# The score mask moves from TensorE to ScalarE, and the weighing of the values to another place in TensorE's order

## The reference

```python
def attn_layer(x, Wqkv, qs, ksc, Wo):        # 16 heads of 64
    q, k, v = split(shift_tokens(x) @ Wqkv)
    q, k = l2norm(q) * qs, l2norm(k) * ksc    # then rotary embedding of both
    # windows of 32 queries against 64 keys (the window before and their own)
    sim = where(mask, -max, (q @ k.T) * 8.0)
    return softmax(sim) @ v @ Wo
def ffn_layer(x, ...):                       # 128 -> 2 x 341 -> 128
    return (a * gelu(gate)) @ W2 + b2        # of the layer norm of shift_tokens(x)
x = attn_layer(x) + x;  x = ffn_layer(x) + x
```

## Time and profile before

| | |
|---|---|
| median of 3 runs | 3490.75 us |
| the profiled execution | 3489.94 us |
| its span | 3488.1 us |
| mean granted TensorE clock | 0.983 |
| PE busy | 3326.3 us (95%) |
| PEld busy | 2681.4 us (77%) |
| DVE busy | 2632.2 us (75%) |
| POOL busy | 2606.3 us (75%) |
| ACT busy | 2200.0 us (63%) |
| mask matmul L903 | 384 of 379 ns |
| split of a weight block on POOL L398 | 72 of 1292 ns |
| gate's table load L639 | 48 of 1283 ns |

### The profile page before, as it was taken

How to read it: one execution, slowest core, us unless ns; L and a number is a source line. 1 busy time by engine, 2 the same in 40 slices (tenths; PEclk the granted TensorE clock), 3 DMA queues, 4 the chain that set the end, 5 groups by cost and what they waited for, 6 DMA issues and landing times.

```text
span 3488.1 us, 149929 instructions
## 1 busy us (share of the span) xinstructions
PE 3326.3 (95%) x63806; PEld 2681.4 (77%) x63806; DVE 2632.2 (75%) x4403; ACT 2200.0 (63%) x4154; POOL 2606.3 (75%) x2894
## 2 busy tenths in 40 slices
PE   6999999999999999999789999999999999999997
PEld 4777778777777777877667777777777778778875
DVE  3777777877787877777458787778787778777773
ACT  3666666666666666666436666666666666666664
POOL 5877787787787777787348778877877877777772
PEclk8999999999999999999879999999999999999998
DMA  2222221221221222221112222212212212221111
GB/s 81 70 55 52 64 56 52 64 61 48 63 62 49 61 62 53 62 63 45 30 26 72 55 54 65 57 51 63 61 47 64 62 51 66 55 56 47 52 46 35
DMA packets 117856, 195.41 MB, mean 56 GB/s; under 512 B 23756, under 2 KB 36552, under 8 KB 117192
## 3 DMA queue, kind: packets, MB, share of 16 engines
q1 hardware_dynamic: 117192, 185.82, 19.6%
HBM read 33.71 MB, written 1.05 MB: 10 GB/s over the span
## 4 chain that ended last, share of the span: by engine, by line
PE 72%; POOL 16%; ACT 6%; issue 3%; DVE 1%; POOLq 0%; DMA 0%; ACTq 0%; SPq 0%; DVEq 0%
PE o_ps L946 10%; PE tr L961 8%; PE s_ps L917 7%; PE tr L930 5%; PE qk_ps L857 5%; POOL rotated L419 5%; PE qk_ps L859 4%; POOL rotated L448 4%; PE qk_ps L858 4%; PE f_ps L1007 4%; PE tr L884 4%; PE tr L857 3%; PE tr L897 3%; POOL prob L425 3%; ACT sq L527 2%
## 5 line engine op out<-in xcount | busy, mean ns | idle before, releaser
L419 POOL TENSOR_TENSOR rotated<-rotated 128x1024 f32<-128x1024 f32 x384 | 917.7, 2390 | 23.7 <-DVE rotated L705 23.7
L448 POOL TENSOR_TENSOR rotated<-rotated,rn 128x1024 f32<-128x1024 f32 x384 | 731.0, 1904 | 30.1
L425 POOL TENSOR_TENSOR prob<-prob,rden 128x512 f32<-128x512 f32 x384 | 436.6, 1137 | 417.2 <-DVE rden L737 413.4
L699 DVE TENSOR_TENSOR rotated<-qk_ps,rot 128x1024 f32<-128x1024 f32 x384 | 469.8, 1223 | 368.0 <-ACT sq L527 362.8
L705 DVE TENSOR_TENSOR rotated<-qk_ps,rot 128x512 f32<-128x512 f32 x768 | 490.4, 679 | 0.0
L917 PEld LDWEIGHTS s_ps<-kt,qt 64*32 64x32 f32 x24576 | 359.5, 107 | 139.6 <-issue 139.6
L712 DVE TENSOR_REDUCE ss_floor<-sq 128x16 f32<-128x1024 f32 x384 | 463.9, 1208 | 0.0
L573 ACT ACTIVATE ot<-o_ps 128x512 f32<-128x512 f32 x384 | 230.6, 601 | 317.4 <-PE o_ps L946 317.4
L917 PE MATMUL s_ps<-kt,qt 64*32 64x64 f32 x24576 | 421.5, 218 | 0.0
L543 ACT ACTIVATE qt<-tr 128x512 f32<-128x512 f32 x384 | 230.1, 599 | 294.5 <-PE tr L884 291.5
L961 PE MATMUL tr<-ot,wo 128*128 128x128 f32 x3072 | 414.6, 278 | 0.0
(11 more groups left out here) (151 smaller groups left out, 6960.5 us busy)
## 6 DMA issues: line engine op xcount, KB each, us to landing
vs<-vn SPq DMA_DIRECT2D x384, 192.0 KB
vs<-vtail SPq DMA_DIRECT2D x384, 64.0 KB, 2.5
vtail<-vn SPq DMA_DIRECT2D x384, 64.0 KB, 2.2
staging<-layer_wqkv_dram SPq DMA_DIRECT2D x72, 256.0 KB, 3.7
wo<-layer_wo_dram SPq DMA_DIRECT2D x12, 512.0 KB, 4.6
xs<-xa SPq DMA_DIRECT2D x48, 128.0 KB, 2.3
fs<-xa SPq DMA_DIRECT2D x48, 128.0 KB, 2.6
xs<-xa SPq DMA_DIRECT2D x48, 127.8 KB, 3.2
```

The lines of the kernel that those rows point to most:

```text
L419: nc.gpsimd.tensor_tensor(rot_c[h], rot_c[h], rot_s[h], ALU.add).then_inc(rot_added, 1)
L425: nc.gpsimd.tensor_tensor(prob[h][:, :, :], prob[h][:, :, :], rden[h][:, :].unsqueeze(2).to_broadcast([P, 2 * PAIRS, KEYS]), ALU.mult).the ...
L448: nc.gpsimd.tensor_tensor(folded, folded, rn[:, :].unsqueeze(2).to_broadcast([P, 2 * UH, DH]), ALU.mult).then_inc(qkn_ready, 1)
L699: nc.vector.tensor_tensor(rot_c[h], src, part(0, 0, DH), ALU.mult)
```

## The change

The mask of all units but the first of each pass is written by ACT: a copy of the bf16 mask, broadcast over the four pairs, into the score bank, behind the exponential of the unit before. PE's `scores` waits for it and adds onto it. The first unit of a pass keeps the mask matmul. On PE the values of unit n-2 are weighed between the key transposes and the values' projection of slot n; before, those of n-1 were weighed at the end of the slot. On ACT the order of a slot becomes exponential, mask, first guess, squares, queries, keys, outputs, values, transposed probabilities. On DVE `add_output` moves behind `differences`.

```diff
         @block.scalar
+            def place_mask(U):
+                act.wait_ge(dif_ready, ONE + U)
+                nc.scalar.activation(s_ps[:, :].rearrange("p (a k) -> p a k", a=PAIRS),
+                                     mask[:, min(U // 2 % TPS, 1), :].unsqueeze(1).to_broadcast([P, PAIRS, 2 * KEYS]), ACT.Copy
+                                     ).then_inc(mask_ready, 1)
...
                     if live(p, n) and after_gated:
                         queries(n)
                         keys(n)
-                    if live(p, n - 2):
-                        outputs(n - 2)
                     if live(p, n - 1):
                         exps(n - 1)
+                    if live(p, n) and n > p * UPP:
+                        place_mask(n)
+                    if live(p, n + 1):
+                        first_guess(n + 1)
+                    if live(p, n + 2):
+                        squares(n + 2)
                     if live(p, n) and not after_gated:
                         queries(n)
                         keys(n)
-                    if live(p, n + 2):
-                        squares(n + 2)
-                    if live(p, n + 1):
-                        first_guess(n + 1)
+                    if live(p, n - 2):
+                        outputs(n - 2)
                     if live(p, n):
                         values(n)
...
         @block.vector
                     if live(p, n + 2):
                         rotate(n + 2)
-                    if live(p, n - 2):
-                        add_output(n - 2)
                     if live(p, n):
                         row_maxima(n)
                         differences(n)
+                    if live(p, n - 2):
+                        add_output(n - 2)
...
         @block.tensor
-            def mask_scores(U):
-                pe.wait_ge(dif_ready, ONE + U)
-                nc.tensor.matmul(s_ps[:, :], ident16[:, :],
-                                 mask[:, min(U // 2 % TPS, 1), :].unsqueeze(1).to_broadcast([P, PAIRS, 2 * KEYS]),
-                                 start=True, stop=False, skip_group_check=True)
-
             def scores(U):
                 h, t = U % 2, U // 2 % TPS
+                if U % UPP == 0:
+                    nc.tensor.matmul(s_ps[:, :], ident16[:, :], mask[:, 0, :].unsqueeze(1).to_broadcast([P, PAIRS, 2 * KEYS]),
+                                     start=True, stop=False, skip_group_check=True)
+                else:
+                    pe.wait_ge(mask_ready, ONE + U - U // UPP)
                 pe.wait_ge(kt_ready, ONE + U + 1)
...
                     if live(p, n):
                         query_heads(p, n)
                         key_heads(p, n)
-                        mask_scores(n)
+                    if live(p, n - 2):
+                        weigh_values(n - 2)
+                    if live(p, n):
                         project_v(n)
                         scores(n)
...
                     if live(p, n - 2):
                         project_out(p, n - 2)
-                    if live(p, n - 1):
-                        weigh_values(n - 1)
```

More of the change, by code:

```diff
@@ L199, in build @@
         s_ready = sem("s_ready")
+        mask_ready = sem("mask_ready")
         max_ready = sem("max_ready")
@@ L488, in _ @@
             for released in (sq_ready, qt_ready, kt_ready, prob_ready, pt_ready, vn_ready, ot_ready, fd_ready, fsq_ready,
-                             fn_hi_ready, gate_ready, guess_ready):
+                             fn_hi_ready, gate_ready, guess_ready, mask_ready):
                 act.sem_inc(released, ONE)
```

## The result

The changed kernel takes 3338.12 us (median of 4 runs, 3337.16 to 3340.91) against 3491.06 us for the kernel before in the same comparison: the ratio is 0.9567, 95% interval 0.955 to 0.9583, 153 us faster. The forecast was 3357 us. The profiled execution took 3337.87 us, its span is 3336.1 us, the mean granted clock 0.984.

What follows compares the result with a forecast made beforehand. It took a ring of waits among ACT, PE and DVE to bound the changed kernel: eight slots sum to 66.33 us against 69.11, 2.78 less, times 48 is 133 us, giving 3357 us; range 3285 to 3445.

Steps and rivals of the forecast that it cites:

- slots 0 and 1: Slots with the gated product and the down projection: forecast at 11.27 and 9.58 us from squares to squares.
- the variances and the spread: FFN work putting 0.92 us on PE in slots 4 and 6, forecast at 7.46 us each.
- the ring: Waits among ACT, PE and DVE, from squares through query copy, scores, maxima, square sums and guess to next squares: 7.15 us.
- the plain slot: One unit's slot without FFN work: forecast at 7.15 us from squares to squares, against 7.29 before.
- rival 1: PE's order alone counts, the guess isn't late: 64.2 us per iteration, 3256 us in all; chance 0.1.
- PE's own sum: PE's work in one slot after the change, if nothing else bound: 6.82 us, 0.47 less than 7.29.
- The centring: Slot 3: centring matmuls on PE take 1.12 us, their ACT copies start at 6.03; slot 8.42 us.
- Guess to squares: On ACT, from the first guess to the next squares: 0.41 us, two small instructions.
- The POOL wait: Probability transposes wait 68.7 us in 80 places for POOL's scaling, 1.43 us per iteration; should vanish.
- The mask's copy: ACT writing the mask into the score bank: taken as 0.60 us, 381 times; no cost in a plain slot.
- Rival 3: Slower: ACT's mask far dearer than a copy; 3668 us at 2.0 us, decides from 1.54 us; chance 0.1.
- Rival 2: The ring is 0.2 us a slot longer than summed, 77 us back: 3434 us; chance 0.15.

Runs made afterwards that it cites:

- e3: The changed kernel with DVE's output addition ahead of the row maxima again, nothing else: 3842.55 us, ratio 1.103 to the kernel before.
- e4: The changed kernel with ACT's first guess moved behind queries and keys, so the squares come ahead of it: 3297.52 us, ratio 0.945 to the kernel before.
- e5: The changed kernel with ACT copying the mask twice, the first time into a spare tile: 3390.53 us.
- e1: The changed kernel with the mask a matmul on PE again, all orders as changed: 3330.85 us, ratio 0.9544 to the kernel before.
- e2: The changed kernel with PE weighing the values of unit n-1 at the slot's end again: 3692.33 us, ratio 1.0583 to the kernel before.

## Why the prediction was right

The span of 8 units, squares to squares, in the changed kernel (squares start at 1099.09 in slot 0, then at 1112.84, 1120.04, 1127.28, 1135.58, 1142.93, 1150.31, 1157.67 and 1165.05):

| slots | forecast | measured |
|---|---|---|
| 0 and 1 (gated, down) | 20.85 | 20.95 |
| 2 | 7.28 | 7.24 |
| 3 (centring) | 8.42 | 8.30 |
| 4 | 7.46 | 7.35 |
| 5 | 7.43 | 7.38 |
| 6 | 7.46 | 7.36 |
| 7 | 7.43 | 7.38 |
| sum | 66.33 | 65.96 |

Against the kernel before the gain isn't spread evenly. There the same distances are, by their medians over the span, 22.16 us for slots 0 and 1, then 7.29, 8.26, 8.21, 7.29, 8.55 and 7.29 for slots 2 to 7. So slots 0 and 1 gain 1.2 us, slot 4 0.9 and slot 6 1.2; slots 2 and 3 stay within 0.05, and slots 5 and 7 are 0.09 us slower. In slots 4 and 6 the variances and the spread, 0.9 us of PE each, used to come on top of the 7.29; now they fill time in which PE would wait for the ring, and half of slot 6's instances lose a POOL wait besides. That is as the prediction summed it (7.46 for these slots, 7.15 for a plain one), though its text dwells on the plain slot.

- **The ring.** Right, in its order and nearly in each term; e3 and e4 cut and loosen it at two places and the time follows. Of the two plain-slot bounds (7.15 ring, 6.82 PE) the larger decided, and rival 1 (3256) did not come. No slot is quite plain: the shortest are slots 1 and 2 with 7.20 and 7.24 us, and slots 5 and 7 have PE's late start in them.
- **PE's own sum.** Mis-sized by 0.09 us: from the output projection to the next full matmul I took 0.91 us from the spread; it is 0.82 (1123.99 to 1124.81 in the changed kernel). That is most of the 0.1 us by which slots 4 and 6 are shorter.
- **The centring.** The copies of the centred values start 5.92 us after the squares (1133.20) and not 6.03, as the two matmuls take 1.02 us for the 1.12 taken. That is most of the 0.12 us of slot 3.
- **Guess to squares.** 0.37 to 0.38 us and not 0.41; why isn't shown. With the two terms above, less the 0.10 us by which slots 0 and 1 are longer than forecast, it makes about the 0.37 us per 8 units, 18 of the 19 us between forecast and result. So the error of 19 us is small partly because the misses are few hundredths each and one goes the other way.
- **The POOL wait.** Right: 68.7 to 4.9 us, since the probabilities are now asked for 2 us after they are scaled.
- **The mask's copy.** 0.591 us for the 0.60 taken, 382 times where the sum counts 381; hidden in most slots, by e5. Rival 3 (slower from 1.54 us) had no ground. What I didn't say is that the copy is also worth nothing: the matmul could stay on PE (e1). The prediction's sum would have told it, as PE waits for the query copy after the matmul's place.
- **Rival 2.** Its 0.2 us a slot did not come; the rotation ends ahead of the maxima by 0.13 us or so in a plain slot, not 0.18, and that was enough.

One thing I didn't count: the low halves on DVE, 1286 ns on the mean before, take 749 ns in the changed kernel. They still run beside POOL's scaling (in 46 of 48 places in both kernels); what most of them no longer meet for long is POOL's addition of the rotary parts, which before still ran for 1.06 us after their start. No gain of time by it is seen: slots 0 and 1 are the ones that came out longer than forecast.

## What to carry to other kernels

When two engines each wait a little for the other, write the ring of waits down with start-to-start distances and compare its length with the busiest engine's own sum; the longer of the two is the slot. The instruction to move is the one that stands ahead of a link of the ring without being one (the addition ahead of the maxima, the guess ahead of the squares); what it waits for, or makes wait, counts for more than its own length (0.28 us for the addition, 0.37 for the guess). And test the parts of an edit alone: here the order made the whole gain, and the edit that gave the change its name costs 65 us alone and about nothing with it.

## What the runs showed of the hardware

The clock: in e3 PE has a hole of 1.6 us ahead of the projection in slots 0, 2, 3 and 6, and one of 0.7 us in slots 4, 5 and 7. With the 0.7 us it was granted full speed in all 132 slots. Of the some 180 slots with 1.6 us, 98 saw the level of 1.2 GHz in place of 2.4 behind the hole (0.83 on the mean of the 10 us stretch shown), so such a hole alone doesn't settle it, and what else it takes isn't shown. In e2 only slot 4 has one, 1.69 us long; the clock fell in 6 of 44 of these, which then took 10.2 us in place of 8.6, and in no other slot. The Trainium skill (TensorE: Matmul & The Clock Gate, "Why this matters for your kernels") warns of idle gaps of about 3 us; these are shorter, and the measurement decides.

DVE and POOL: DVE's low halves (one instruction with two tiles of SBUF as input) take 0.70 us at their shortest and 1.92 us in the median of e4. In the rows of e4 they are issued at 1020.41, while POOL adds the rotary parts until 1021.79, and they end 0.54 us after that; POOL's scaling, issued at 1021.74, takes 1.50 us in place of 1.04. In the kernel before, where (at 1010.37) the addition ended 1.06 us after the low halves' start, they took 1.61 us; in the changed kernel (at 1033.50) it ends 0.22 us after it, and they take 0.77. In all three they end 0.54 or 0.55 us behind POOL's addition. The Trainium skill (SBUF — State Buffer, "Terms") says that the two engines share a port pair that one instruction holds to its end while the other is blocked; the trace agrees: DVE's instruction waits for POOL's addition, and POOL's next instruction, the scaling, waits for DVE's. Neither was tried by itself.
